# Re-ordering the drain of a product-key attention kernel: tile 31 ahead of tile 30's last gaps

## What is computed

```
xn = layernorm(x)
s  = attention(xn)          # three branches (blocks of 4 rows, 64 selected rows, windows of 32),
                            # gated, times Wo, half residual, normalised over the 128 columns
sx, ix = top_k(sim[0], 16)  # per row and head (8 heads): 32 keys in each of two halves
sy, iy = top_k(sim[1], 16)
scores, pk = top_k(sx[:, None] + sy[None, :], 16)
h  = gelu(xn . W_down[pk]) * softmax(scores)
f  = sum_k h[k] * W_up[pk[k]]
out = x + s * silu(f)
```

## Time and profile before

| | us |
|---|---|
| median of 3 runs (lowest, highest) | 285.66 (285.27, 288.36) |
| the profiled execution's own time | 286.57 |
| its span, first to last instruction | 284.8 |
| busy in the span: VectorE, TensorE, ScalarE, GpSimd | 266.3, 241.8, 237.7, 228.8 |
| mean granted TensorE clock | 0.986 |
| last sorting instruction of tile 31 ends, about | 260.3 |

### The profile page before, as it was taken

One profiled execution on the slowest core, in us unless ns is written; L12 is line 12 of the kernel. 1 busy time (PEld: TensorE's weight loads), 2 busy tenths in 40 slices (PEclk: granted clock), 3 DMA queues, 4 the chain that ended last, 5 costly groups with the idle time before them and its releaser, 6 DMA issues.

```text
span 284.8 us, 7972 instructions
## 1 busy us (share of the span) xinstructions
PE 241.8 (85%) x1564; PEld 176.8 (62%) x1564; DVE 266.3 (94%) x2573; ACT 237.7 (83%) x1064; POOL 228.8 (80%) x351
## 2 busy tenths in 40 slices
PE   7899797896888898889897989798979897988792
PEld 7666243584676566656675666576667565756591
DVE  5899989999999999999999999999999999997474
ACT  2455768699888998899889988999899989997832
POOL 7888610478688879997999899979997999798791
PEclk9999999999999999999999999999999999999959
DMA  7920000000000000100010001000100010001002
GB/s 170 279 72 2 0 1 0 2 1 1 3 1 0 5 1 3 39 1 2 1 39 2 1 2 39 2 3 1 38 2 2 1 37 3 3 2 38 1 2 74
DMA packets 11235, 6.29 MB, mean 22 GB/s; under 512 B 1457, under 2 KB 10674, under 8 KB 11186
## 3 DMA queue, kind: packets, MB, share of 16 engines
q1 hardware_dynamic: 9858, 5.12, 6.8%
q10 hardware_dynamic: 1328, 0.66, 1.2%
HBM read 3.67 MB, written 2.10 MB: 20 GB/s over the span
## 4 chain that ended last, share of the span: by engine, by line
DVE 61%; PE 18%; issue 7%; ACT 7%; POOL 6%; POOLq 0%; DVEq 0%
DVE rest L1120 23%; DVE top L1109 13%; DVE top L1129 13%; DVE last L1153 6%; PE t_bank L1409 4%; PE s_bank L1446 2%; DVE slot_gap L1138 2%; POOL squareT L487 1%; PE sim L1460 1%; PE f_bank L1453 1%; PE c_bank L1453 1%; PE scratch L1440 1%; POOL past L472 1%; DVE slot_gap L1144 1%; PE c_bank L1524 1%
## 5 line engine op out<-in xcount | busy, mean ns | idle before, releaser
L1120 DVE MATCH_REPLACE8 rest<-top,sim 128x32 f32<-128x32 f32 x512 | 85.9, 180 | 0.1
L1129 DVE MAX8 top<-rest 128x8 f32<-128x32 f32 x512 | 53.5, 177 | 0.7
L808 ACT ACTIVATE prob<-drop 128x50 f32<-128x50 f32 x232 | 53.4, 254 | 0.0
L1109 DVE MAX8 top<-sim 128x8 f32<-128x32 f32 x496 | 51.0, 178 | 0.4 <-PE sim L1460 0.4
L808 ACT ACTIVATION_READ_ACCUMULATOR prob<-drop 128x1 f32 x232 | 48.5, 212 | 0.0
L487 POOL TENSOR_TENSOR squareT<-sideT 100x512 bf16<-100x512 bf16 x31 | 32.2, 1040 | 13.8 <-ACT sideT L722 13.8
L1120 DVE MATCH_VALUE_LOAD rest<-top,sim 128x8 f32 x512 | 41.0, 80 | 0.3
L472 POOL TENSOR_TENSOR past<-gap,last 128x400 f32<-128x400 f32 x31 | 26.8, 863 | 10.4 <-DVE last L1153 10.4
L1460 PE MATMUL sim<-sim_w,xT_all 128*128 128x512 f32 x64 | 33.4, 603 | 0.8 <-ACT xT_all L758 0.8
L494 POOL TENSOR_TENSOR drop<-gap,out_by 128x400 f32<-128x400 f32 x31 | 32.0, 1032 | 1.7 <-ACT out_by L713 1.7
L1478 PE MATMUL t_bank<-gaps_of,topT 128*128 128x200 f32 x128 | 29.3, 351 | 2.0 <-ACT topT L727 2.0
(11 more groups left out here) (276 smaller groups left out, 727.9 us busy)
## 6 DMA issues: line engine op xcount, KB each, us to landing
out<-y_sb SPq DMA_DIRECT2D x7, 256.0 KB, 2.3
x_sb<-in_L_attn_hidden_states SPq DMA_DIRECT2D x2, 256.0 KB, 4.1
fwq_sb<-in_L_ffn_Wq ACTq DMA_DIRECT2D x2, 256.0 KB, 6.0
x_sb<-in_L_attn_hidden_states SPq DMA_DIRECT2D x1, 512.0 KB, 5.8
wc_sb<-in_L_attn_Wc SPq DMA_DIRECT2D x1, 256.0 KB
out<-last_y SPq DMA_DIRECT2D x2, 128.0 KB, 1.8
wo_in<-in_L_attn_Wo SPq DMA_DIRECT2D x1, 192.0 KB
keys_sb<-in_L_ffn_keys ACTq DMA_DIRECT2D x1, 128.0 KB, 3.6
```

The costliest lines, as they stand in the source:

```text
L808: last = nc.scalar.activation(prob[d][:, h, :], drop[:, h, :], ACT.Exp, scale=-1.0, accum_out=den[d][:, h:h + 1])
L1109: last = nc.vector.max(top[d][:, v, 0:8], sim_bank[d][:, bass.ts(v, KEYS)])
L1120: last = nc.vector.match_replace(out=rest[:, v, :], in_to_replace=top[d][:, v, 0:8], in_values=sim_bank[d][:, bass.ts(v, KEYS)], imm_value ...
L1129: last = nc.vector.max(top[n % 2][:, v, 8:16], rest[:, v, :])
```

## The change

It touches the drain and three places of the turns.

- VectorE sorts tile 31 to its end before it takes tile 30's last gaps; `maxima` stand ahead of `late_gelu`. Further on it takes over from GpSimd the inverse row sums times gates and the scaling of the block probabilities (`scale_blocks`), and for batch 6 one product of half `f` and the normalised attention (`late_half`); tile 30 gets the instruction that only tile 31 had (`keep_last`, twice). The statistics of batch 7's first half stand between the weighing of tiles 30 and 31.
- Tiles 30 and 31 get buffers of their own (`last_drop`, `last_prob`, `last_wgts`, sums), tile 31 `last_sideT` and `last_squareT`, and waits on the shared buffers are dropped.
- Tile 28 is summed by VectorE too (`summed`), so its exponentials are one activation. Tiles 28 and 29 are no longer added up by GpSimd: TensorE does it in four products, as for tiles 30 and 31.
- GpSimd keeps the scaling of the window probabilities, `weigh` for tiles 28 and 29, one product for batch 6 (`late_product`), and the variances; the addition of batch 5's input comes behind tile 30's `past`, and that of batch 6 behind the variances.
- ScalarE copies tile 31's gaps before tile 30's signs, and does two and two window exponentials with the transposed sides of tile 30 between them. Batch 6's `silu_parts` (three activations) is replaced by `late_tanh` (two).
- TensorE adds the residual rows of batch 7 as one product of 256 columns for each half (`add_rows`: identity times xn) where four products with `off_mean` stood.

```diff
         def summed(n):
-            return n >= TILES - 3
+            return n >= TILES - 4
...
             past_of(TILES - 2)
+            add_input(B - 3)
             drop_of(TILES - 3)
+            square_of(TILES - 2)
             weigh(TILES - 4)
...
+            pool.wait_ge(rgate_done, B)
+            nc.gpsimd.tensor_tensor(p_win[:, :, :], p_win[:, :, :],
...
+            def late_product():
...
+                pool.wait_ge(f_out, B - 1)
+                pool.wait_ge(y_step, 2 * (B - 2) + 1)
+                pool.wait_ge(y_done, B - 2)
+                nc.gpsimd.tensor_tensor(y3[:, :, :], tanh1_f[:, :, :], y1[:, :, :], ALU.mult).then_inc(y_step, 1)
...
-            add_input(B - 2)
+            late_product()
             pool.wait_ge(s_done, B - 1)
             last_variances(0)
             last_variances(1)
+            add_input(B - 2)
...
+            def late_half():
...
+                nc.vector.scalar_tensor_tensor(y1[:, :, :], last_f[:, :].rearrange("p (t d) -> p t d", t=TB), 0.5,
+                                               s_norm[(B - 2) % 2][:, :, :], ALU.mult, ALU.mult).then_inc(y_step, 1)
...
+            def scale_blocks():
...
+                nc.vector.tensor_scalar(p_cs[:, 0:BLOCKS], p_cs[:, 0:BLOCKS], rgate[:, TB:TB + 1], None, ALU.mult)
...
+            last_gaps(n - 1)
+            maxima(b)
             late_gelu()
...
             gaps_of_pairs(n)
             gaps_of_thirds(n)
             last_gaps(n)
+            last_past_of(n)
+            invert_sums(n - 3)
+            late_half()
             inverse_row_sums(b)
...
+            def add_rows(k):
...
+                mm(last_out[k][:, bass.ds(j * D, LAST * D)], ident[:, :],
...
             b = B - 1
+            block_scores(b)
             top_columns(TILES - 1)
...
+            transpose_sides(TILES - 1)
             count_places(TILES - 2)
...
+            add_rows(0)
+            expert_weights(TILES - 4)
+            count_places(TILES - 1)
             transpose_window_probs(b)
             transpose_block_probs(b)
...
             attention_out(b, range(LAST))
+            attention_out(b, range(LAST, TB))
             expert_weights(TILES - 3)
...
             expert_weights(TILES - 2)
```

More of the change, by code:

```diff
@@ L233, in program @@
         wgt2 = [sb(f"wgt2_{i}", [P, 2, CANDS]) for i in range(2)]
-        last_drop = sb("last_drop", [P, HEADS, CANDS])
+        last_drop = [sb(f"last_drop{i}", [P, HEADS, CANDS]) for i in range(2)]
+        last_prob = [sb(f"last_prob{i}", [P, HEADS, CANDS]) for i in range(2)]
+        last_wgts = [sb(f"last_wgts{i}", [P, HEADS, CANDS]) for i in range(2)]
+        last_den, last_rden = ([sb(f"{n}{i}", [P, HEADS]) for i in range(2)] for n in ("last_den", "last_rden"))
+        last_sideT = sb("last_sideT", [P, L], BF16)
+        last_squareT = sb("last_squareT", [P, L], BF16)
         last_y = sb("last_y", [P, TB, D])
@@ L417, in place_constants @@
                 pool.wait_ge(xn_done[0], 3)
+                nc.gpsimd.memset(last_sideT[96:P, :], 1.0)
                 place(1, nc.gpsimd.memset(sideT[96:P, :], 1.0))
@@ L631, in turn @@
                     add_quarters(n - 4)
-                    if b >= 2:
+                    if b >= 2 and n < TILES - 1:
                         add_input(b - 2)
@@ L851, in silu_parts @@
                     act.wait_ge(y_step, 2 * b - 1)
-                f_v = (e_bank if b < B - 2 else last_f)[:, :].rearrange("p (t d) -> p t d", t=TB)
+                f_v = e_bank[:, :].rearrange("p (t d) -> p t d", t=TB)
                 nc.scalar.activation(tanh_f[:, :, :], f_v, ACT.Tanh, scale=0.5).then_inc(tanh_done, 1)
@@ L899, in last_norms, with window_exps @@
                 half.then_inc(last_norm, 1)
-            def window_exps(b):
+            def window_exps(b, tiles=range(TB)):
                 act.wait_ge(max_done, b + 1)
-                for g in range(TB):
+                for g in tiles:
                     nc.scalar.activation(p_win[:, g, :], s_bank[:, bass.ts(g, WKEYS)], ACT.Exp,
@@ new lines, in keep_last @@
+            def keep_last(m):
+                k = m - (TILES - LAST)
+                dve.wait_ge(count_ready, m + 1)
+                nc.vector.scalar_tensor_tensor(last_drop[k][:, :, :].rearrange("p h c -> p (h c)"),
+                                               (t_bank if k else f_bank)[:, 0:HEADS * CANDS], OUT_SCALE,
+                                               gap[m % 4][:, :, :].rearrange("p h c -> p (h c)"),
+                                               ALU.mult, ALU.max).then_inc(last_kept, 1)
@@ L1500, in count_places @@
                     pe.wait_ge(last_square, 1)
-                dst = f_bank if n < TILES - 1 else t_bank
+                dst, one, two = (f_bank, sideT, squareT) if n < TILES - 1 else (t_bank, last_sideT, last_squareT)
                 for k in range(HEADS // 2):
                     o = dst[:, bass.ts(k, TWO)]
-                    mm(o, sideT[0:TWO + 1, bass.ts(k, P)], count_s[0:TWO + 1, :], start=True, stop=False)
-                    last = mm(o, squareT[0:TWO, bass.ts(k, P)], count_q[0:TWO, :], start=False, stop=True)
+                    mm(o, one[0:TWO + 1, bass.ts(k, P)], count_s[0:TWO + 1, :], start=True, stop=False)
+                    last = mm(o, two[0:TWO, bass.ts(k, P)], count_q[0:TWO, :], start=False, stop=True)
                 last.then_inc(count_ready, 1)
@@ L1626, in attention_out @@
                 for j in tiles:
-                    o = (out_bank if b < B - 1 else last_out[j // LAST])[:, bass.ts(j, D)]
-                    mm(o, xT_all[:, bass.ts(b * TB + j, P)], off_mean[:, :], start=True, stop=False)
+                    if b < B - 1:
+                        o = out_bank[:, bass.ts(j, D)]
+                        mm(o, xT_all[:, bass.ts(b * TB + j, P)], off_mean[:, :], start=True, stop=False)
+                    else:
+                        o = last_out[j // LAST][:, bass.ts(j, D)]
+                        if j == LAST:
+                            add_rows(1)
                     if j == 0:
@@ L1631, in attention_out @@
                         mm(o, pT_cs[0:SELECT_K, 1, :], vwc[0:SELECT_K, 1, :], start=False, stop=False)
-                    last = mm(o, pT_win[:, j, :], vww[:, j, :], start=False, stop=True)
+                    last = mm(o, pT_win[:, j, :], vww[:, j, :], start=False,
+                              stop=(b < B - 1 or j % LAST == LAST - 1))
                 if TB - 1 in tiles:
```

140 lines of the change are left out of this document (76 added, 64 removed).

## The result

The changed kernel takes 283.99 us (median; lowest 283.33), the kernel before 286.62 beside it: a ratio of 0.9889, with an interval of 0.9843 to 0.9936. One of the four executions of the changed kernel was a slow one of 541.67, which the median counts and the ratio leaves out; the other three took 283.33 to 284.64 (median 283.34). The prediction was 283.4 us, a ratio of 0.992 to the median that it started from; 283.99 lies in its range. The gain of 1.1% lies at the edge between the two cases to which the prediction gave 0.72 (within 1%) and 0.24 (faster than that). The profiled execution took 284.64, with a span of 282.8 (before: 286.57 and 284.8).

The account below looks back on a forecast made before the run. The prediction took the drain to be bounded by a chain through tile 31, with TensorE's last work at half clock. Span 284.8 - 2.25 = 282.55; the gain off the median 285.66 gave 283.4 us, range 281.9 to 285.8.

Parts of the forecast that it names:

- The clock: TensorE in the drain stays at 2.4 GHz; last weights end at 275.2, not 278.27: gain 3.07, half from the clock.
- rivals 3 and 4: Clock falls again near 270 for 6.8 us, no gain, 285.7 (0.1); or falls about 267, stays to the end, 288.8 (0.04).
- Tile 31's gaps, 1.53: ScalarE in the drain writes tile 31's gaps by 262.60 instead of 264.13, a gain of 1.53 us.
- `past`, 2.65 kept: VectorE's stretch from tile 31's gaps to the end of `past` stays 2.65 us, ending at 265.26.
- Weighing, gain left 1.54: VectorE's weighing of tiles 30 and 31 ends at 274.08, not 275.62, after 0.68 given back to first-half statistics.
- Rival 2: VectorE and GpSimd slow each other; both weighings take 1.21, 1.6 us less gain, 285.0; chance 0.1.
- VectorE's new work: Between `past` and tile 31's count: half product 0.67, four small scalings 0.85 (0.4 to 1.4), ending 0.5 us before the count.
- Weights of tile 28, 0.9: TensorE's four new products (eight instructions) ahead of tile 31's count take 0.9 us, bounds 0 and 2.1.
- The last 4.24 stay: From TensorE's last weights to the last `last_y` stays 4.24 us; last piece at 279.44 rather than 282.51.
- The stores, 3.07 to 2.25: Last two pieces wait until batch 6's store, written later by GpSimd, lands at 279.8; gain shrinks from 3.07 to 2.25.
- rival 1: The last store does not wait, GpSimd or batch 6's landing being 0.8 us sooner; whole 3.07 gained, 282.6; chance 0.2.
- Start of the kernel, 0: One more GpSimd memset at the kernel's start costs 0, at most 0.5 us.

Follow-up runs that it names:

- order-only runs: Kernel before with tile 31's order changed, tile 28 by one exponential: drain 26.51, ratio 1.0009; same with tile 28's sum ahead of tile 31's gaps: 24.06, 0.9983.

## Why the prediction was right, and where not

That 283.99 lies so near 283.4 is in part luck. The forecast took its gain of 2.25 off a median of 285.66, where the old kernel stood at 286.62 beside the changed one, while the drain gave 0.87 more than forecast.

*The clock.* Right: 1.00 through 270 to 277, and so rivals 3 and 4 did not come. Held by itself, it is 1.42 at the weights, near the half of 3.07 that the prediction gave it, and 1.02 at the end.

*Tile 31's gaps, 1.53.* Measured 1.38, on its way as predicted (one exponential, then the copy of the top scores). But the prediction let each earlier step pass through to the end, as if the chain through tile 31 bounded the drain alone. The order-only runs refute that for the kernel before: the gaps at +3.13 brought nothing with GpSimd's queue as it was. Only with the relief of GpSimd is the chain the bound, and then all of it passes (0.48 to 0.47).

*`past`, 2.65 kept.* This step failed in size: `past` took 0.57, not 1.21, so from gaps to `past` it was 2.01. *Weighing, gain left 1.54.* The same: 0.57 twice instead of 0.84 and 0.81, gain 2.34. The prediction priced VectorE's products by rows of before, in which GpSimd was at work when they started, and asked only whether they would get slower. GpSimd's rows of before:

```profile
265.32 1.04 POOL L487 TENSOR_TENSOR squareT<-sideT 100x512 bf16<-100x512 bf16 x1 [1.31 <-ACT sideT L722]
...
272.35 1.27 POOL L578 TENSOR_TENSOR y<-tanh_f,half_f 128x512 f32<-128x512 f32 x1
273.70 1.48 POOL L585 TENSOR_TENSOR y<-y,s_norm 128x512 f32<-128x512 f32 x1
```

They end at 266.36, 273.62 and 275.18, and `past` and the two weighings 0.42 to 0.44 behind them. So the 0.84 and 0.81, which the prediction took for undisturbed, were lengthened as well. After, tile 30's weighing has GpSimd idle beside it, `past` starts ahead of GpSimd's square, and tile 31's weighing as GpSimd's product ends. For `past` the order alone does that: 0.57 and 0.58 in the order-only kernels, whose weighings mostly keep their 0.8. Rival 2 is right as a mechanism and wrong in sign: adding GpSimd's work back costs tile 30's weighing 0.48.

*VectorE's new work.* `late_half` 0.69, predicted 0.67. The four small instructions took 0.27, 0.15, 0.84 and 0.24, 1.5 in all and over the upper end of 1.4, since the third stood beside GpSimd's `p_win`. It cost nothing: the second `last_drop` followed the first, and the count was there.

*Weights of tile 28, 0.9.* Measured 1.04 for the eight instructions, without a wait ahead of them; count at +8.46, predicted +8.79.

*The last 4.24 stay.* They became 4.58 (+14.90 to +19.48). The prediction took TensorE's weights as the start of that stretch; it starts with the second means, which beside GpSimd's addition took 1.22. So 0.67 gained at the weights was 0.33 at the last piece.

*The stores, 3.07 to 2.25.* Right in kind: the first last piece was ready at +18.23 and went at +19.30, behind batch 6's landing. The size was off: batch 6 was written at +16.96, not +17.82, because the second statistics, behind shorter weighings, ended 0.7 earlier than forecast and the addition took 1.26, not 1.48. The wait cost 0.31, not 0.82. That the drain lost just the 3.07 of rival 1 is chance: its mechanism, a store that holds nothing, is refuted by the run in which the store was freed.

*Start of the kernel, 0.* No cost can be seen: in the changed kernels without a dip in the head the drain begins at 259.30 to 259.51, before at 259.63.

So the drain is 22.05 against 22.92: VectorE's lengths gave more than was forecast, the held means took half of it back, and the store cost 0.5 less. In the time of the kernel the dips in the head, which come with the old drain and the new, hide most of that.

## What to carry to other kernels

A chain of waits names the bound only as long as the next queue is further behind: before adding up gains along one chain, ask of every engine with a full queue when it would end if the chain were gone. Here that queue was GpSimd's, and reordering alone put a new wait in front of it.

A duration read from a trace holds for its neighbourhood: where a change empties or fills GpSimd beside VectorE, price VectorE's products with two inputs in SBUF both ways, and look which of the two engines starts first. And where single dips of the clock move the start of a stretch, measure the stretch from a row ahead of the change, not the span.

## What the runs showed of the hardware

VectorE's products of 128x400 with two inputs in SBUF took 0.57 to 0.58 where GpSimd was idle, at the last 0.06 of an instruction or started behind them, and 0.63 to 1.21 where GpSimd's instruction had started first. Then VectorE's ended close behind it: `past` of before at 266.78 (GpSimd 266.36), the weighing with the added work at 271.67 (GpSimd 271.23), the 128x2 `nmr` at 277.76 (GpSimd 277.73), the finishing product at 277.23 (GpSimd 276.94). It looks like a wait and not a slower pace: `nmr` took 1.22 for two numbers per partition, and 0.16 with GpSimd's addition out of its way. GpSimd waits too: its variance of 128x2 took 0.60 beside tile 31's weighing, 0.19 elsewhere.

With one input in PSUM VectorE was not held: `last_drop` of before, 128x400, took 0.57 from 270.70 on the earlier trace rows, all but the last 0.03 of it beside a weighing that GpSimd had begun earlier:

```profile
270.38 0.86 POOL L500 TENSOR_TENSOR wgt<-prob,rden 128x400 f32<-128x400 f32 x1
```

The Trainium skill (SBUF — State Buffer, SBUF: two separate sides) calls the shared pair of ports an exclusive lock: whichever starts first has it for its whole instruction, and the other blocks. The rows with two inputs in SBUF agree. One row goes beyond two inputs: the scaling of `p_cs`, with one tensor in SBUF, took 0.84 for 128x128 beside `p_win` (until 268.52), although its own start is recorded 0.05 ahead of GpSimd's, and 0.24 for 64x64 behind it. The Trainium skill (SBUF — State Buffer, SBUF: two separate sides) also names VectorE instructions in a mode of two ports as blocking and blocked; whether this scaling is one, no run here tells.

In the head of some executions TensorE's granted clock averaged 0.66 over 5 us, so part of it at its lower level of 1.2 GHz, and stayed at 1.00 in others with the same instructions there; what decides it no run here shows.
